# One-hot rows of the position counts: 26 compares on GpSimd in place of two on VectorE

## What is computed

```python
e = layernorm(x)                                        # 4096 x 512
h = einsum(rmsnorm(e, g_res), W_in) + b_in
bidx = cumsum(mask) - 1                                 # positions where a piece ends
boundary_mask = zeros(4096).at[bidx].set(1)
plug = clip(cumsum(boundary_mask) - 1, 0, 3201)         # for each row of x a row of ctx
s = linear_recurrence(rmsnorm(ctx, g_init)[:, :512])    # s[t] = a*s[t-1] + u[t]
x = x + h + s[plug]
x = x + gelu(layernorm(x) @ w1 + b1) @ w2 + b2          # 512 -> 2048 -> 512
```

## Time and profile before

| | us |
|---|---|
| three timed runs | 856.88, 859.49, 860.17; median 859.49 |
| profiled execution | 857.83, of which the span in the trace 856.0 |
| busy in the span: TensorE / VectorE / ScalarE / GpSimd | 832.5 / 318.5 / 292.7 / 266.5 |
| VectorE, the three one-hot instructions together | 5.6 |

### The profile page before, as it was taken

The page is one execution under the profiler, slowest core; times in us unless marked ns, Lnnn a source line. Parts: engine busy times, 40 slices in busy tenths (PEclk is TensorE's granted clock), DMA queues, the critical chain, the costliest instruction groups (busy, mean ns, idle before and its releaser), DMA issues.

```text
span 856.0 us, 10869 instructions
## 1 busy us (share of the span) xinstructions
PE 832.5 (97%) x3774; PEld 684.9 (80%) x3774; DVE 318.5 (37%) x523; ACT 292.7 (34%) x506; POOL 266.5 (31%) x290
## 2 busy tenths in 40 slices
PE   5989989999999999999999999999999999999998
PEld 5777868788888888888888887888888888888886
DVE  5887863434333241524251423234112411241112
ACT  4674435542342226122522343213222222222221
POOL 5272574980163005320532035202500250012000
PEclk9998999999999999999999999999999999999999
DMA  9865896241113312150216021402400140010001
GB/s 239 288 168 161 316 269 234 76 138 34 65 59 87 83 49 74 47 123 0 74 60 159 0 74 49 96 0 72 77 1 1 49 86 12 0 49 1 1 1 49
DMA packets 36168, 73.17 MB, mean 85 GB/s; under 512 B 5764, under 2 KB 6788, under 8 KB 34248
## 3 DMA queue, kind: packets, MB, share of 16 engines
q1 hardware_dynamic: 27452, 61.54, 22.1%
q0 software_dynamic: 4608, 8.39, 6.1%
q10 hardware_dynamic: 4080, 2.89, 1.2%
HBM read 48.92 MB, written 23.89 MB: 85 GB/s over the span
## 4 chain that ended last, share of the span: by engine, by line
PE 85%; DVE 5%; POOL 3%; DMA 3%; issue 2%; ACT 2%; SPq 0%; POOLq 0%; DVEq 0%; ACTq 0%
PE acc L786 14%; PE acc L788 14%; PE acc L787 14%; PE h_bank L786 13%; PE h_bank L788 13%; PE h_bank L787 13%; PE t_bank L829 2%; DVE cl L949 1%; DMA x_next<-scan_table,idx 1%; DMA ch<-in_ctx_dram 1%; DMA win_raw<-in_L_xattn_W_in_dram 1%; POOL x_next L508 1%; POOL x_next L513 1%; PE t_bank L805 1%; DVE h_lo L937 1%
## 5 line engine op out<-in xcount | busy, mean ns | idle before, releaser
L1149 DVE TENSOR_TENSOR h_lo<-g_f,h_hi 128x512 fp32r<-128x512 f32 x128 | 100.8, 788 | 452.0 <-ACT g_f L725 452.0
L723 ACT ACTIVATE h_hi<-h_bank,b_c 128x512 fp32r<-128x512 f32 x128 | 87.8, 686 | 434.8 <-PE h_bank L788 429.9
L786 PE MATMUL h_bank<-xt_hi,w_hi 128*128 128x512 f32 x512 | 202.2, 395 | 0.0
L786 PE MATMUL acc<-w_hi,h_hi 128*128 128x512 f32 x512 | 200.0, 391 | 0.0
L788 PE MATMUL h_bank<-xt_hi,w_lo 128*128 128x512 f32 x512 | 199.6, 390 | 0.0
L787 PE MATMUL h_bank<-xt_lo,w_hi 128*128 128x512 f32 x512 | 199.6, 390 | 0.0
L787 PE MATMUL acc<-w_lo,h_hi 128*128 128x512 f32 x512 | 199.5, 390 | 0.0
L788 PE MATMUL acc<-w_hi,h_lo 128*128 128x512 f32 x512 | 199.5, 390 | 0.0
L787 PEld LDWEIGHTS h_bank<-xt_lo,w_hi 128*128 128x128 f32 x512 | 96.2, 188 | 20.9 <-issue 1.2
L786 PEld LDWEIGHTS h_bank<-xt_hi,w_hi 128*128 128x128 f32 x512 | 96.2, 188 | 20.7 <-issue 1.2
L788 PEld LDWEIGHTS h_bank<-xt_hi,w_lo 128*128 128x128 f32 x512 | 96.2, 188 | 20.0
(11 more groups left out here) (147 smaller groups left out, 737.1 us busy)
## 6 DMA issues: line engine op xcount, KB each, us to landing
x_next<-x_part SPq DMA_DIRECT2D x8, 1024.0 KB, 4.8
out_dram<-x_cur SPq DMA_DIRECT2D x32, 256.0 KB, 2.1
w_raw<-in_L_ffn_w_dram SPq DMA_DIRECT2D x6, 1024.0 KB, 10.3
scan_table<-cl SPq DMA_DIRECT2D x6, 896.0 KB
cl<-in_ctx_dram SPq DMA_DIRECT2D x5, 1024.0 KB
ch<-in_ctx_dram SPq DMA_DIRECT2D x20, 256.0 KB, 2.9
xa_even<-in_x_dram SPq DMA_DIRECT2D x16, 256.0 KB, 4.8
xa_odd<-in_x_dram SPq DMA_DIRECT2D x16, 256.0 KB, 6.8
```

The lines of the kernel that those rows point to most:

```text
L723: act.activation(h_hi[:, m % HB, :], h_bank[m % 2][:], ACT.Gelu, bias=b1_c[:, m:m + 1])
L786: nc.tensor.matmul(dst, a_hi, b_hi, start=first, stop=False)
L1149: dve.tensor_tensor(h_lo[:, m % HB, :], g_f32[:], h_hi[:, m % HB, :].bitcast(F32), ALU.subtract).then_inc(h_split, 1)
```

## The change

The two broadcast compares on VectorE are gone. GpSimd makes the same `oh_p` with 26 instructions, one for each column of `pos_p`: each compares the 128 numbers of `iota_p` with one number for each partition. Thirteen stand in GpSimd's turn 8 and thirteen in its turn 9, each lot behind that turn's `times_g_init` and ahead of what else the turn has. A semaphore `pos_ready`, raised when `pos_p` is written, is what GpSimd waits for; VectorE waits for the same one where it had waited for its own. `oh_q` stays on VectorE and goes from turn 8 to turn 9. TensorE's wait for three signals stays.

```diff
+            def one_hots_p(j0, j1):
+
+                pool.wait_ge(pos_ready, 1)
+                for j in range(j0, j1):
+                    ins = pool.tensor_scalar(oh_p[:, j, :], iota_p[:], pos_p[:, j:j + 1], 1.0, ALU.is_equal, ALU.mult)
+                ins.then_inc(onehots, 1)
...
                 if 9 <= t <= 12:
                     times_g_init(1, t - 9, cl_next)
+                if t in (8, 9):
+                    one_hots_p((t - 8) * MJ // 2, (t - 7) * MJ // 2)
                 if t == 18:
...
-                step(dve.tensor_copy(pos_p[:], ib[:]))
+                dve.tensor_copy(pos_p[:], ib[:]).then_inc(pos_ready, 1)
+                dve.wait_ge(pos_ready, 1)
...
-            def one_hots_p(j0, j1):
-                n = j1 - j0
-                dve.tensor_tensor(oh_p[:, j0:j1, :], pos_p[:, j0:j1].unsqueeze(2).to_broadcast([P, n, P]),
-                                  iota_p[:].unsqueeze(1).to_broadcast([P, n, P]), ALU.is_equal).then_inc(onehots, 1)
...
-                if t == 8:
+                if t == 9:
                     one_hots_q()
-                if t == 9:
-                    one_hots_p(0, MJ // 2)
-                if t == 10:
-                    one_hots_p(MJ // 2, MJ)
```

More of the change, by code:

```diff
@@ L261, in xattn_ffn @@
         onehots = sem("onehots")
+        pos_ready = sem("pos_ready")
         counted = sem("counted")
```

## The result

The changed kernel takes 872.66 us (median of four, 871.65 to 874.13) against 858.84 us of the kernel before beside it: 13.8 us slower, a ratio of 1.0161 (95% interval 1.0147 to 1.0174). The forecast was 862.1 us with a range up to 866.5. The direction and the places of the loss were as forecast. The size was not, and the measured time is outside the range.

A forecast was written before the change was run, and what follows sets the result against it. TensorE was taken as the bound, waiting 4.2 us in the first stage, with VectorE not the bound there. Terms -0.25, +5.9, -0.2, -2.05, +0.4 and -0.4 gave +3.4 on 858.7: 862.1 us, range 859.3 to 866.5.

The forecast's parts named there:

- the price of a compare: One of 26 new GpSimd compares of 128 columns: 0.29 us, from the select's 0.25 plus 0.04.
- The upper end of 0.43 us: Far end for a compare on GpSimd, from the multiplication of two tensors at 2.1 ns a column; 26 make 11.2 us.
- The sum: All terms of the forecast together: +3.4 us on a start of 858.7 us, giving 862.1 us.
- the first wait: TensorE's wait for `n_rows` of tile 14: 1.69 us becomes 1.45, a term of -0.25 us.
- The count: TensorE's instruction that wants all of `oh_p`: waits until 61.6, 5.9 us, where it waited for nothing.
- `row_tot`: TensorE's third wait in the first stage: 2.26 us becomes 0.2, a term of -2.05 us.
- the debt of block 1: Late statistics of tile 19 delay `scales`, `rc_next` and block 1's last scan, making the carry later: +0.4 us.
- the clock: TensorE's granted clock falls in the new wait, costing 2.8 us in place of 3.2: a term of -0.4 us.
- VectorE is not the bound at 47 to 50: TensorE takes a tile every 3.2 us without idle time while VectorE makes one-hot rows; hidden-bound rival, chance 0.03.
- The 2.80 us of idle time: GpSimd's wait for `mv_a`; with 1.5 us saved in `mr_a` it pays for the first thirteen compares, 0.25 us left over.
- The rival "slower compares": GpSimd as the bound: each 0.01 us of a compare costs 0.26 us; at 0.43 us, 865.7 us; chance 0.30.
- the old slow stretch: TensorE at granted clock 0.50 for 6.5 us, until about 72.5, after the `row_tot` wait: costs 3.2 us.

The follow-up runs named there:

- the small kernel: Kernel that copies x to the output and times fourteen instruction forms, six each, on GpSimd with VectorE idle; the compare took 0.717 us, no ratio.
- the zeroing: Changed kernel with compares over 16 of 128 columns, GpSimd first zeroing the rest of `oh_p` in turn 3: 864.31 us, ratio 1.0073.
- the order experiment: Changed kernel with each lot of thirteen compares moved to the end of its GpSimd turn, behind the scales: 875.72 us, ratio 1.019.
- the spread kernel: Kernel before with `row_tot` ahead of the scans, `oh_p` in four VectorE instructions in turns 9 to 12, count one turn later: 856.42 us, ratio 0.9978.
- three exchanges of order: Each on the kernel before: one-hot instructions behind statistics, 858.23 us; `rc_next` ahead of the scale of tiles 18 and 19, 858.20; `row_tot` ahead of scans, 857.65.
- two of them together with the spread: Kernel before with `row_tot` ahead of the scans, `oh_p` in four instructions, count one turn later, and `rc_next` earlier on GpSimd: 854.31 us, ratio 0.9958.

## Why the prediction was wrong

**The step that failed is the price of a compare**, "I take 0.29 us, near the select, which it resembles". It is 0.695 us in the kernel and in the small kernel. The upper end of 0.43 us was no bound either: it came from the slope of a multiplication of two tensors, 2.1 ns a column, and a compare with one tensor input costs 3.3 ns a column. The row nearest in shape gave 0.25 us and that slope 0.43, and the unknown operation lay outside both. The 0.04 us for the column of numbers had no row; against a constant it is 0.08. The argument "only one tensor is read" was the wrong one, since with that same input two multiplications took 0.37 us and the compare 0.72. The Trainium skill ("GPSIMD Engine Reference", 3.1 Elementwise) puts a body of at most two operations at 1.03 cycles an element. The copies in the small kernel agree, with 0.83 ns a column (292 ns for 128, 609 for 512), one cycle at the 1.2 GHz of the same page (1. Specifications). The compare does not: its 3.3 ns are four such cycles, and the measurement decides.

**The sum held with the measured price.** Its slope was 26 instructions, with no slack left: 3.4 + 26 x (0.695 - 0.29) = +13.9 us against 13.8 measured. With one operation it gave 869.6 against 869.87. With 0.32 us and the zeroing's 1.8 us it gives +6.0 against +5.9.

That it holds to 0.1 us in the changed kernel is in part luck, since four of its terms were off and cancel. With the measured price the first wait is as forecast (+5.0 us). The count comes out at +10.6 against 11.2, `row_tot` at -1.65 against -2.05, the debt of block 1 at +1.1 against +0.4, and the clock at -1.0 against -0.4 (below).

Point by point, in the changed kernel:
- VectorE is not the bound at 47 to 50: right, tile 13 did not move (50.50 against 50.45).
- `oh_q` next on VectorE at 46.7, behind the pair, holding the first compare until 48.8: right. It started at 46.77, and the compare lost 0.8 us.
- GpSimd: pair until 47.95 (48.0), `scales` 1.73 us and `rc` 2.15 us behind the first lot without a gap: right. The 2.80 us of idle time paid for part of the lot as said, and the order experiment shows it from the other side.
- The wait for `row_tot` becomes 0.2: it is 0.61.
- The debt of block 1, +0.4: it is 0.92 + 0.17 = 1.1 us. The chain was the right one and the slack that I gave it too large. The same chain took back over 2 us in the spread kernel, and moving `rc_next` gave them again.
- The clock, -0.4: partly right. It fell in the first wait, 6.7 us long where 1.45 had been forecast, and not at the count; what was slowed was about 3.4 us of work after 72.24 and the transpose at 60.56, so some 2 us were lost and not the 2.8 taken (1.12 against 0.49 us for the transpose, and 4.83 against 3.50 us from the count to the next transpose). The 0.6 us at the transpose are hidden in the wait for the count, which is shorter by them. What went with the old slow stretch is 3.0 us (6.14 from `count_before` to the next transpose, against 3.28, and 0.1 behind).

The waits of the changed kernel are 6.71 + 10.56 + 0.61 + 0.17 + 0.92 = 19.0 us against 4.2; less 1.0 us of slow clock this is 13.8. The mark behind the first stage, GpSimd's first addition of `b2`, comes 14.1 us later (173.95 against 159.83), and the end of the span 15.2 us. The last 1.1 us arose in the feed-forward part of this execution and are not in the medians.

**The rival "slower compares"** was the mechanism that occurred, with its place, its sign and its 0.26 us for 0.01; its price of at most 0.43 us cut it off at 865.7 us.

What remains open: why the clock fell after a wait of 1.7 us in one execution and not in that of the kernel before, and stayed up after one of 2.1 us in another. As the mean clock differs between executions of one and the same kernel, a single trace does not tell what a wait will do to it; no run here shows what decides. A difference of 1 to 2 us between medians in the last experiments can be the clock's in part.

## What to carry to other kernels

When an instruction moves to GpSimd and the trace has no row of this operation there, neighbours of the same shape do not bound it: select 0.29, two multiplications 0.37, compare 0.72 us for the same 128 columns. Give such a price a wide upper end, or measure it in a kernel of a few microseconds first, above all where it is multiplied by 26.

A queue with little idle time ahead of a wait pays for each instruction in full. Count what stands ahead of the waiting engine's release, not the engine's busy share (31% here).

Taking away a stop shows the next one. Here, in a stage where each chain was a microsecond or two behind another, three exchanges of order brought 0, 0 and 1 us each alone, and two of them together with the spread count 4.3 us.

## What the runs showed of the hardware

- On GpSimd a compare or a subtraction with a column of numbers, 128 columns with a second operation, takes 0.72 us, whatever the output type; with one operation 0.60, with a constant 0.64; two multiplications take 0.37, a select or a copy 0.29 (the small kernel).
- VectorE's instruction with two SBUF inputs can go in between two of GpSimd's queued compares and hold the rest for its whole length (11.58 us instead of 9.82 for a lot).
- The granted clock stayed at 0.50 through waits, from before 60 to 75.6 us in the changed kernel, and still through the count and the first half of the tile behind it.
- Executions of one kernel differ in it: the kernel without most of its compares had a mean granted clock of 0.998 in four executions and 0.993 to 0.995 in six, which took 1 to 4 us longer.
